# Two PSUM banks each for the gate and value matmuls of the last layer's experts, with the sigmoid and the products taken by halves

## What is computed

```
for e in range(N_EXPERTS):                      # 8 experts, D = 256, H = 512
    tok, slot = jnp.nonzero(top_ids == e, size=CAPACITY, fill_value=(N, 0))
    w = probs_pad[tok, slot][:, None]
    xin = x_pad[tok]
    a = xin @ W[e]
    b = xin @ V[e]
    y = a * (b * jax.nn.sigmoid(b)) @ W_out[e]
    out = out.at[tok].add(y * w)
```

## Time and profile before

| What | Value |
|---|---|
| Median of three runs | 1535.52 us (1534.79 to 1538.48) |
| Span of the profiled execution | 1563.1 us |
| TensorE busy, of the span | 1312.0 us (84%) |
| VectorE busy | 806.2 us (52%) |
| ScalarE busy | 485.7 us (31%) |
| GpSimd busy | 490.2 us (31%) |
| Mean granted TensorE clock | 0.935 of 2.4 GHz |
| Stretch of the last layer's expert tiles in the span | 1354.8 to 1548.9 us |

### The profile page before, as it was taken

How to read it: one execution, slowest core, us unless ns; L and a number is a source line. 1 busy time by engine, 2 the same in 40 slices (tenths; PEclk the granted TensorE clock), 3 DMA queues, 4 the chain that set the end, 5 groups by cost and what they waited for, 6 DMA issues and landing times. The chain is left out here.

```text
span 1563.1 us, 30738 instructions
## 1 busy us (share of the span) xinstructions
PE 1312.0 (84%) x9996; PEld 1047.9 (67%) x9996; DVE 806.2 (52%) x2646; ACT 485.7 (31%) x1103; POOL 490.2 (31%) x465
## 2 busy tenths in 40 slices
PE   5987899967898888798896899976888888889995
PEld 3766688955565556687885677754555555778885
DVE  6786344445676665232453466653555665344442
ACT  3654111114544542010110345443545443111000
POOL 1243522232134224224122346532222332322221
PEclk9999899979999999899998889898999999899998
DMA  9000333321013002643542200000000010634523
GB/s 308 4 29 29 128 114 120 97 83 41 22 45 130 15 29 73 219 143 103 157 136 91 69 14 1 1 1 20 8 28 29 29 36 29 218 82 121 125 45 81
DMA packets 85602, 119.38 MB, mean 76 GB/s; under 512 B 11184, under 2 KB 63152, under 8 KB 85200
## 3 DMA queue, kind: packets, MB, share of 16 engines
q1 hardware_dynamic: 45408, 50.86, 10.7%
q10 hardware_dynamic: 25856, 35.14, 7.1%
q0 software_dynamic: 14224, 31.92, 7.1%
HBM read 81.86 MB, written 38.13 MB: 77 GB/s over the span
## 5 line engine op out<-in xcount | busy, mean ns | idle before, releaser
L1250 PEld LDWEIGHTS bank<-f_xT,f_up 128*128 128x128 f32 x2144 | 262.1, 196 | 8.6 <-DVE f_xT L1122 3.3
L1250 PE MATMUL bank<-f_xT,f_up 128*128 128x128 f32 x2144 | 263.3, 279 | 2.1 <-DVE f_xT L1122 2.1
L385 DVE TENSOR_REDUCE mha_nmax<-bank 128x2 f32<-128x512 f32 x256 | 170.2, 687 | 158.4 <-PE bank L506 116.9
L1259 PE MATMUL bank<-f_down,f_hT 128*128 128x256 f32 x832 | 201.7, 386 | 15.8 <-DVE f_hT L1156 15.8
L506 PE MATMUL bank<-l_took,mha_q 32*128 32x256 f32 x1024 | 152.5, 416 | 62.3 <-DVE mha_nmax L385 47.0
L291 ACT ACTIVATE l_took<-bank 128x512 f32<-128x512 f32 x256 | 139.2, 598 | 156.5 <-PE bank L514 138.3
L1259 PEld LDWEIGHTS bank<-f_down,f_hT 128*128 128x128 f32 x832 | 151.2, 192 | 39.5 <-issue 22.0
L1017 POOL DMA_INDIRECT yout<-f_y,f_to x66 | 81.1, 1229 | 269.4 <-DVE f_y L1190 121.5
L506 PEld LDWEIGHTS bank<-l_took,mha_q 32*128 32x128 f32 x1024 | 92.1, 191 | 103.1 <-DVE mha_nmax L385 66.9
L514 PE MATMUL bank<-l_took 32*128 32x256 f32 x1024 | 151.4, 414 | 2.5 <-DVE l_took L394 2.0
L1060 ACT ACTIVATE f_hT<-bank,f_b 128x128 f32<-128x128 f32 x148 | 46.3, 364 | 316.8 <-PE bank L1250 316.8
(11 more groups left out here) (291 smaller groups left out, 2358.5 us busy)
## 6 DMA issues: line engine op xcount, KB each, us to landing
f_up<-in_W ACTq DMA_DIRECT2D x26, 512.0 KB, 4.8
f_xt<-rows SPq DMA_DIRECT2D x88, 132.0 KB
f_down<-in_W ACTq DMA_DIRECT2D x20, 512.0 KB
f_xt<-rows SPq DMA_DIRECT2D x20, 264.0 KB, 2.7
ring<-yout SPq DMA_DIRECT2D x8, 512.0 KB, 4.3
mha_ctxT<-in_ctxT SPq DMA_DIRECT2D x16, 256.0 KB, 2.8
f_up<-in_W SPq DMA_DIRECT2D x6, 512.0 KB
f_up<-in_V ACTq DMA_DIRECT2D x6, 512.0 KB, 3.9
```

The costliest lines, as they stand in the source:

```text
L385: vector.tensor_reduce(nmax[:, p, :, at], ps_s[n % 2][:, :].rearrange("p (k s) -> p k s", s=S), AX.X, ALU.min).then_inc(max_ready, 1)
L1250: ins = pe.matmul(into, up[q][i][:, c, m * P:(m + 1) * P], xT[:, c, :], start=c == 0, stop=c == DC - 1)
L1259: ins = pe.matmul(ps_y[:, 0:D], hT[:, m, :], down[q][:, m, :], start=m == 0, stop=m == HC - 1)
```

## The change

In layer 3, chunks m = 0, 1 of V go to bank 7 and m = 2, 3 to bank 2; chunks m = 0, 1 of W go to bank 6 and m = 2, 3 to bank 3. Banks 2 and 3 belong to the router, which is done by then. `h_done` follows each half, four times a tile instead of twice, so every count of it becomes `UPS` = 4 per tile. ScalarE takes the sigmoid in two instructions of 256 columns, each after its half of V; VectorE takes the product of value and gate in two instructions of 256 columns, each after its half of the sigmoid, and then the product with W in two, each after its own half of W. In layers 0 and 1, `UPS` is 2, and every count and bank stays as it was; a wait of ScalarE only moves by a line in the text.

```diff
+    ps_w, ps_v = [PS[6], PS[3]], [PS[7], PS[2]]
+    UPS = len(HALVES) * UP
...
-                    act.wait_ge(at.h_done, PRIMED + 2 * j + 1)
                     if GLU:
-                        act.wait_ge(at.gated, PRIMED + j)
-                        act.activation(gate[:, :, :].rearrange("p c r -> p (c r)"), ps_h[1][:, :],
-                                       ACT.Sigmoid).then_inc(at.gate_ready, 1)
+                        act.wait_ge(at.gated, PRIMED + 2 * j)
+                        for i, (m, _) in enumerate(HALVES):
+                            act.wait_ge(at.h_done, PRIMED + UPS * j + i + 1)
+                            act.activation(gate[:, m:m + 2, :].rearrange("p c r -> p (c r)"), ps_v[i][:, 0:2 * R],
+                                           ACT.Sigmoid).then_inc(at.gate_ready, 1)
                     else:
+                        act.wait_ge(at.h_done, PRIMED + UPS * j + 1)
...
-                vector.wait_ge(at.h_done, PRIMED + 2 * j)
+                vector.wait_ge(at.h_done, PRIMED + UPS * j)
...
-                        flat = lambda a: a[:, :, :].rearrange("p c r -> p (c r)")
-                        vector.wait_ge(at.gate_ready, PRIMED + j + 1)
+                        part = lambda a, m: a[:, m:m + 2, :].rearrange("p c r -> p (c r)")
                         vector.wait_ge(at.y_done, PRIMED + j)
-                        vector.tensor_tensor(flat(hT), ps_h[1][:, :], flat(gate), ALU.mult).then_inc(at.gated, 1)
-                        vector.wait_ge(at.gated, PRIMED + j + 1)
-                        vector.wait_ge(at.h_done, PRIMED + 2 * j + 2)
                         for i, (m, _) in enumerate(HALVES):
-                            part = flat(hT)[:, m * R:(m + 2) * R]
-                            vector.tensor_tensor(part, ps_h[0][:, m * R:(m + 2) * R], part, ALU.mult).then_inc(at.hT_ready[i], 1)
+                            vector.wait_ge(at.gate_ready, PRIMED + 2 * j + i + 1)
+                            vector.tensor_tensor(part(hT, m), ps_v[i][:, 0:2 * R], part(gate, m), ALU.mult).then_inc(at.gated, 1)
+                        for i, (m, _) in enumerate(HALVES):
+                            vector.wait_ge(at.gated, PRIMED + 2 * j + i + 1)
+                            vector.wait_ge(at.h_done, PRIMED + UPS * j + 2 + i + 1)
+                            vector.tensor_tensor(part(hT, m), ps_w[i][:, 0:2 * R], part(hT, m), ALU.mult).then_inc(at.hT_ready[i], 1)
...
-                            into = ps_h[i][:, m * R:(m + 1) * R] if GLU else ps_h[m // 2][:, m % 2 * R:(m % 2 + 1) * R]
+                            into = ((ps_w, ps_v)[i] if GLU else ps_h)[m // 2][:, m % 2 * R:(m % 2 + 1) * R]
...
-                            if GLU and m == HC - 1 or not GLU and m % 2:
+                            if m % 2:
                                 ins.then_inc(at.h_done, 1)
```

More of the change, by code:

```diff
@@ L1159, in expert @@
                             marked(j + 1)
-                        vector.wait_ge(at.h_done, PRIMED + 2 * j + 2)
+                        vector.wait_ge(at.h_done, PRIMED + UPS * j + 2)
                         for m in HALVES[1]:
```

## The result

The changed kernel took 1507.9 us (median of 4 runs, 1502.89 to 1510.33) against 1535.15 us for the kernel before (4 runs): a ratio of 0.9839, interval 0.9805 to 0.9872, or 27 us less. The forecast was 1516.5 us with a range of 1513 to 1524: the right way, but the gain is larger than the range allowed.

A forecast was written before the change was run, and what follows sets the result against it. TensorE was taken to set the pace, waiting once a tile for hT's first half in layer 3's experts. Terms 15.5 + 0.6 + 3.4 + 0.2 - 0.7 = 19.0 us; 1535.5 - 19.0 = 1516.5 us, range 1513 to 1524.

The forecast's parts named there:

- The price of an ordinary tile: Layer 3's experts: a tile falls from 6.14 to 5.52 us, priced from layer 0's loop; 25 tiles give 15.5 us.
- The order of events: Within a tile, from V's start: gate products at 1.67 and 2.56 us, W products at 2.98 and 3.77, down matmuls at 3.79.
- The bound for unshortened halves: If halving shortened no instruction, hT's first half comes at 4.11 us against 4.34, still 0.23 us a tile gained.
- The price of the split: VectorE's two half products cost 0.15 us a tile more than one whole, hidden by W's matmuls; uncovered, 4.5 us.
- the term of tiles 2 to 4: First expert of layer 3: ScalarE's table load starts 0.89 us earlier, each tile gains 1.14 us, three tiles 3.4 us.
- The second term: First tile of layer 3's experts: the same wait for hT's first half goes away, 0.6 us.
- The loading tiles: One tile where ScalarE's queue issues weight loads before its sigmoid: halves bring the down matmuls 0.2 us earlier.
- The rows of the next tile: Next tile's row load arrives late beside weight loads, at most 0.3 us each; 0.7 us taken off the gain.
- rival 1: Waiting for the next tile's rows replaces the removed wait; 0.3 us in every tile, gain 10, 1525.5 us; chance 0.10.
- Rival 2: TensorE's clock falls in the denser loop, 5.5 us more per slow tile; five make 1544 us; chance 0.03.
- Rival 3: hT's first half still comes after the transposes, so TensorE's wait stays: within 0.3% of 1535.5 us; chance 0.05.

The follow-up runs named there:

- The three partial kernels: Three kernels: W alone in halves, V alone in halves, and the whole change with TensorE awaiting both halves of hT; ratios 0.9978, 0.9965 and 0.9977.
- the quarters: Changed kernel with each sigmoid and each product in two instructions of 128 columns, signals unaltered; ratio 0.9866.
- the kernel with the order alone: Kernel before, with only ScalarE's two waits in layer 3 swapped: gate's buffer first, V's matmuls second; ratio 0.9985.
- the one with the old order: Changed kernel with ScalarE's two waits put back: first half of V, then the gate's buffer; ratio 0.9857.
- the second comparison: Changed kernel, unaltered, timed and profiled again beside the kernel before, also unaltered: 1515.0 us against 1532.9, ratio 0.9894.
- the third: Changed kernel, unaltered, timed once more against the kernel before: 1511.5 us against 1533.7, ratio 0.9849.

## Why the prediction was wrong, and where it was right

**The price of an ordinary tile** held: 5.52 us, and 5.51 to 5.52 in nearly all of them. Layer 0's loop was the right measure (the earlier trace rows shows the first and the ninth copy, so eight intervals of 3.731 us), and the recorded idle time of 0.39 us was too low, as it said. **The order of events** held: the products with W within 0.1 us, the gate products 0.16 us earlier than worked out (1.51 and 2.41 for 1.67 and 2.56), without effect on the down matmuls, which start behind the transposes. The bound for unshortened halves, 4.11 us, is 4.04 by its own terms (2.06 + 0.60 + 0.12 + 0.69 + 0.42 + 0.15); both lie under 4.34. The three partial kernels come out at the times which the same sum gives them (5.98 against 5.99; 6.14 against 6.14; 6.14 against 6.10). **The price of the split**: one product takes 0.692 us for 512 columns, 0.424 for 256 and 0.286 for 128, so two halves cost 0.16 us more than the whole, and no tile is longer for it, since it lies under W's matmuls even when it is doubled. The Trainium skill (VectorE: DVE Perf Modes, "The TRN2 errata") states such a fixed latency for each instruction and advises 512 elements or more. The trace agrees on the price; that it isn't on the path here is what the quarters show.

**The step that failed** is the term of tiles 2 to 4, "After the change the load can start 0.89 us earlier, 1366.10". I took the load of ScalarE's table to follow V's matmuls as before and moved it by half of V. But the diff also puts the wait for the gate's buffer first, and the load goes ahead of V altogether, as the kernel with the order alone and the one with the old order show. These tiles gained 3 x 1.75 = 5.25 us instead of 3.4; of the 0.61 us a tile that I missed, 0.38 is the order (5.90 to 5.52) and 0.23 that the halves follow each other faster than I added them up (6.13 to 5.90).

The second term is "The first tile: the same wait, 0.6 us". Between the first profiles that tile gained 2.0 us, of which 1.4 is TensorE's clock, not the change (V and W in 6.78 us at a granted clock of 0.54 before, 5.38 us at 0.70 after); the 0.6 that is left agrees with the forecast by luck, since V and W were slow enough there to cover the table load. Between the second ones V and W took about as long (5.22 and 5.46 us), and it gained 1.5 us (8.77 to 7.25): there the load held TensorE in the first tile too, and the order alone brought it to 7.72. The down matmuls of the first tile in the two profiles of before, 7.38 us (load hidden) and 6.97 us (load on the path) after V:

```profile
1363.14 1.97 PE L1259 MATMUL bank<-f_down,f_hT 128*128 128x256 f32 x8 [0.39 <-DVE f_hT L1156]
```

```profile
1330.46 1.97 PE L1259 MATMUL bank<-f_down,f_hT 128*128 128x256 f32 x8 [1.53 <-DVE f_hT L1156]
```

Between the second profiles the two terms together were 2.8 us too small, and the other tiles gave 14.6 instead of 15.0.

**The loading tiles.** The 0.2 us of the earlier trace rows came out differently in each profile: that tile gained 1.0 us between the first two (6.83 to 5.81) and lost 0.2 between the second two (6.34 to 6.53). The sigmoid stands behind the load issues on ScalarE's queue, and the issue of the W load there took 0.49 to 1.69 us from tile to tile. The longest, in the changed kernel's second profile:

```profile
1400.25 3.73 PE L1254 MATMUL bank<-f_xT,f_up 128*128 128x128 f32 x32
...
1400.85 1.69 ACTq L1026 DMA_DIRECT2D f_up<-in_W  x1
...
1403.33 0.66 ACT L1059 ACTIVATE f_gate<-bank 128x256 f32<-128x256 f32 x2 [6.23 <-PE bank L1254]
...
1404.97 1.97 PE L1263 MATMUL bank<-f_down,f_hT 128*128 128x256 f32 x8 [0.78 <-DVE f_hT L1160]
```

**The rows of the next tile** became a wait as rival 1 had it, but only beside weight loads, and for less than the 0.7 us allowed: in the first profile one tile shows it, behind one at which weights load. The chain of the changed kernel there, and the transposes that waited:

```profile
1400.81 4.94 DMA f_xt<-rows
1405.75 0.04 issue
1405.79 0.44 PE bank L1237 x2
```

```profile
1405.79 0.44 PE L1237 MATMUL bank<-consts,f_xt 128*128 128x128 f32 x2 [0.23 <-DMA f_xt<-rows]
```

The load took 4.94 us here, longer than the 4.68 which bounded it. TensorE's recorded wait is 0.23 us, and this tile takes 5.97 us, 0.45 more than the others.

**Rival 2, the clock,** did not come: from the second tile to the last, the changed kernel's granted clock is 1.00, the upper level, in all three profiles, with TensorE busy throughout:

```profile
1324.23:1483.38 159.15, 158.86 (x1212) 152.64 (x1211) 90.89 (x313) 24.30 (x60) 45.04 (x29) 1.00 0.44 98
```

The columns are those of the earlier trace rows. **Rival 3** is out: in ordinary tiles the down matmuls start 0.21 to 0.22 us after the transposes do, and the idle time between them is nothing.

**The range** was missed by more than these terms. With the two terms right the forecast would have been a gain of some 22 us, which is what the stretches show, and which the range of 1513 to 1524 still held by half a us. The rest is scatter, of which I had allowed 2 us: the range started from 1535.5, where later executions of the same kernel have a median of 1533.3, and the first four of the changed kernel fell low (1507.9, against 1510.6 over 16, which is itself below 1513 because of that start). The scatter comes ahead of layer 3's experts: over ten profiles taken after the first, their first up matmul started between 1310.2 and 1331.3 us with nothing changed before it that runs there.

What makes that work scatter wasn't tried, but the record shows what goes with it. The profiled execution with the start at 1310.2 (the kernel with the order alone) has a mean granted clock of 0.949, the one at 1331.3 (W alone in halves) has 0.934; among the executions of the kernel before, one of 1521.1 us shows 0.948 and one of 1545.1 shows 0.929. The six changed executions of the second comparison average 0.9355, those of the third 0.940, which goes with 17.9 us in the one and 22 in the other. Where both kernels show 0.940, five executions of the kernel before took 1529.3 to 1534.2 us and two of the changed one 1507.8 and 1510.3, 23.5 us apart in the mean. Whether the clock makes the scatter, or both follow something else, stays open; the first profile of before (1355.8 us, 0.935) lies far from the others at its clock.

## What to carry to other kernels

If a neighbouring loop already has the structure that a change brings, price the change by that loop's steady interval: here it gave 5.52 us to the hundredth, while the idle time in the profile, counted from a modelled end, said 0.39 us where 0.62 were gained. Where two waits follow each other under one engine, halving one of them can be worth little: here 0.15 us and 0 of the 0.62 that both gave. And read a diff for the order of its waits too: the table load, an instruction that the program text does not have, stood behind the first of two waits only.

## What was not expected

The table load runs between two waits that the program has for one sigmoid, so swapping two lines took 1.13 us off each of three tiles. The same DMA issue on ScalarE's queue took 0.49 us in one tile and 1.69 in another, and it holds whatever is behind it there, here the sigmoid of the first tile of an expert.
